# Another order for splits, first step and routing in a decoder-layer kernel, and a scratch of running sums whose half steps are 8 KB pieces

## What is computed

```
proj = x @ W_in.T                      # val, gate, B, C (32 heads x 128), dt (32)
dt = softplus(dt + dt_bias);  ld = dt * -exp(A_log);  cum = cumsum(ld, axis=1)
M = (C @ B.T) * exp(where(mask, cum_l - cum_m, -inf))
Y = M @ val + ... + D * val;  out = (Y * silu(gate)) @ W_out.T
```

```
scores = sigmoid(xt @ gate.T);  _, sel = top_k(scores + expert_bias, 2)
hs = silu(xt @ shared_w1.T) * (xt @ shared_w3.T);  out = hs @ shared_w2.T  (+ routed experts)
```

## Time and profile before

| | |
|---|---|
| median of 3 runs | 790.55 us (790.09 to 791.51) |
| the profiled execution: its own time | 791.8 us |
| the profiled execution: its span | 789.9 us |
| PE busy | 740.9 us (94%) |
| DVE busy | 578.2 us (73%) |
| ACT busy | 455.0 us (58%) |
| POOL busy | 353.6 us (45%) |
| mean granted PE clock | 0.970 |

### The profile page before, as it was taken

One profiled execution on the slowest core, in us unless ns is written; L12 is line 12 of the kernel. 1 busy time (PEld: TensorE's weight loads), 2 busy tenths in 40 slices (PEclk: granted clock), 3 DMA queues, 4 the chain that ended last, 5 costly groups with the idle time before them and its releaser, 6 DMA issues. The chain is left out here.

```text
span 789.9 us, 17296 instructions
## 1 busy us (share of the span) xinstructions
PE 740.9 (94%) x5910; PEld 409.1 (52%) x5918; DVE 578.2 (73%) x1127; ACT 455.0 (58%) x890; POOL 353.6 (45%) x412
## 2 busy tenths in 40 slices
PE   8799599999999999999999999999589999888996
PEld 3455265555655556555565555656324444344554
DVE  5586376686776867868668688796688899847776
ACT  7554155754454664444475554555347788647775
POOL 3864435493342745434358675454213311230343
PEclk9999799999999999999999999999879999889999
DMA  6755114113632232621313334330040000000001
GB/s 208 268 114 178 26 47 90 54 53 78 172 82 53 53 86 51 155 94 53 92 49 99 56 68 104 63 74 2 14 190 15 23 22 23 14 2 1 28 28 54
DMA packets 34282, 57.91 MB, mean 73 GB/s; under 512 B 7040, under 2 KB 11904, under 8 KB 33664
## 3 DMA queue, kind: packets, MB, share of 16 engines
q1 hardware_dynamic: 33664, 57.08, 27.3%
q10 hardware_dynamic: 576, 0.31, 0.1%
HBM read 54.10 MB, written 2.36 MB: 71 GB/s over the span
## 5 line engine op out<-in xcount | busy, mean ns | idle before, releaser
L287 POOL TENSOR_TENSOR cum_rows<-cum_rows,cum_t 128x512 f32<-128x512 f32 x128 | 136.3, 1075 | 205.9 <-DMA cum_rows<-cum_scratch 205.9
L786 PE MATMUL pring<-xt_hi,w_hi 128*128 (+1 forms) x576 | 173.2, 383 | 10.1 <-POOL xt_lo L279 9.0
L786 PE MATMUL pring<-xt_lo,w_hi 128*128 (+1 forms) x576 | 172.5, 381 | 0.0
L786 PE MATMUL pring<-xt_hi,w_lo 128*128 (+1 forms) x576 | 172.2, 381 | 0.0
L647 DVE TENSOR_TENSOR bt<-pring,bt 128x512 f16<-128x512 f32 x128 | 88.1, 689 | 73.9 <-ACT bt L444 73.6
L444 ACT CAST bt<-pring 128x512 f16<-128x512 f32 x128 | 74.7, 584 | 112.7 <-PE pring L786 112.7
L651 DVE TENSOR_TENSOR ct<-pring,ct 128x512 f16<-128x512 f32 x128 | 88.3, 690 | 53.6 <-ACT ct L448 53.1
L828 PEld LDWEIGHTS pscore<-ct,bt 128*128 128x128 f16 x1536 | 96.5, 98 | 32.9 <-issue 5.5
L828 PE MATMUL pscore<-ct,bt 128*128 128x128 f16 x1536 | 107.3, 220 | 1.5 <-issue 1.4
L448 ACT CAST ct<-pring 128x512 f16<-128x512 f32 x128 | 74.9, 585 | 53.0 <-PE pring L786 52.9
L1127 DVE TENSOR_REDUCE mx<-bank_at 128x4 f32<-128x512 f32 x128 | 83.6, 689 | 15.8 <-PE bank_at L1203 14.7
(11 more groups left out here) (153 smaller groups left out, 953.9 us busy)
## 6 DMA issues: line engine op xcount, KB each, us to landing
cum_rows<-cum_scratch SPq DMA_DIRECT2D x32, 1024.0 KB, 8.2
w_raw<-in_w_in SPq DMA_DIRECT2D x35, 256.0 KB, 6.6
q_rows<-in_xt SPq DMA_DIRECT2D x4, 512.0 KB, 11.0
acc<-in_x SPq DMA_DIRECT2D x1, 2048.0 KB, 7.3
vals<-in_vals SPq DMA_DIRECT2D x16, 128.0 KB, 2.1
out<-acc SPq DMA_DIRECT2D x8, 256.0 KB, 2.1
w_raw_e<-in_w_up SPq DMA_DIRECT2D x1, 1024.0 KB, 5.0
w_raw_e<-in_w_gate SPq DMA_DIRECT2D x1, 1024.0 KB, 7.0
```

Source lines behind the costliest of these rows:

```text
L287: nc.gpsimd.tensor_tensor(rows[:, par, :, q], rows[:, par, :, q], own, ALU.subtract).then_inc(sem("since"), 1)
L786: mm = nc.tensor.matmul(bank[name][:], w[:, c, k, cols], x[:, k, bass.ds(n % TB, 1), :].rearrange("p o n -> p (o n)"), start=(i == 0), sto ...
```

## The change

On the host nothing changes. In the kernel these things do:

- The scratch has another layout: block, half step, sequence, head, position. A half step's rows are then one contiguous piece of 8 KB, where they were four pieces of 2 KB. It is stored by 4 transfers per block, one for each sequence (16 in all), where it was stored by 2 transfers in all.
- SP issues the stores of blocks 1 to 3 ahead of the load of `acc` (2 MB), no longer waits for `rows1` there, and waits for all stores.
- Weight chunk 1 is split by ACT (high part only) and DVE (`first_low`), as chunk 0 was; ACT does so ahead of the softplus. POOL takes chunk 5 ahead of the first exponents.
- In the first step PE does pair 0 ahead of the turn of the sums, and pair 3 ahead of the widths of blocks 1 and 2; the width of block 3 comes behind `turn_values`. ACT and DVE have another order of the same work.
- POOL's `split_x(3)` stands ahead of `exponents(2, 0)`.
- In the experts, PE turns the logits ahead of `shared_up(0, 1)`, and DVE's `gate_shared(0)` stands in the middle of the routing.

```diff
-        cum_d = nc.dram_tensor("cum_scratch", (TB, NB * H, L), F32, kind="Internal").ap()
+        cum_d = nc.dram_tensor("cum_scratch", (TB, 2 * GROUPS, NB, 4, L), F32, kind="Internal").ap()
...
             def store_sums(t0, t1):
-                sp.dma_start(cum_d[t0:t1].rearrange("t p n -> p t n"),
-                             dz[:, 0, t0 * L:t1 * L].rearrange("p (t n) -> p t n", n=L)).then_inc(sem("cum_out"), 16)
+                for t in range(t0, t1):
+                    for b in range(NB):
+                        sp.dma_start(cum_d[t, :, b].rearrange("g q n -> g (q n)"),
+                                     dz[b * H:b * H + H, 0, t * L:t * L + L]).then_inc(sem("cum_out"), 16)
             def load_rows(tb, quad, par):
-                src = cum_d[bass.ds(tb, 1)].rearrange("t (b h) n -> (t b) h n", h=H)[:, bass.ds(4 * quad, 4), :]
-                sp.dma_start(rows[:, par].rearrange("p b q n -> p b (q n)"),
-                             src.rearrange("b q n -> b (q n)").partition_broadcast(P)).then_inc(sem(f"rows{par}"), 16)
+                src = cum_d[bass.ds(tb, 1), bass.ds(quad, 1)].rearrange("t g b q n -> (t g) (b q n)")
+                sp.dma_start(rows[:, par].rearrange("p b q n -> p (b q n)"),
+                             src.rearrange("o n -> (o n)").partition_broadcast(P)).then_inc(sem(f"rows{par}"), 16)
             sp.wait_ge(sem("dt_cum"), 1)
             store_sums(0, 1)
-            sp.wait_ge(sem("cum_out"), 16)
+            sp.wait_ge(sem("cum_out"), 16 * NB)
...
-            sp.wait_ge(sem("rows1"), 16)
+            sp.wait_ge(sem("dt_cum"), TB)
+            store_sums(1, TB)
             sp.dma_start(acc[:], io["x"]).then_inc(sem("in_x"), 16)
             sp.dma_start(expo[:], io["expo"]).then_inc(sem("in_x"), 16)
-            sp.wait_ge(sem("dt_cum"), TB)
-            store_sums(1, TB)
-            sp.wait_ge(sem("cum_out"), 32)
+            sp.wait_ge(sem("cum_out"), 16 * NB * TB)
...
-            pool.wait_ge(sem("w_ready"), 1)
-            for c in range(1, 5):
+            pool.wait_ge(sem("w_ready"), 2)
+            for c in range(2, 6):
                 lo_part(0, c)
             pool.wait_ge(sem("cum_t"), 1)
-            exponents(0, 0, {1: 5, 3: 6})
+            exponents(0, 0, {3: 6})
...
             split_x(2)
+            split_x(3)
             exponents(2, 0)
-            split_x(3)
...
             split_x(0)
             hi_part(0, 0, True)
+            hi_part(0, 1, True)
...
             softplus(slice(0, L), 0)
-            hi_part(0, 1, True)
             hi_part(0, 2, True)
...
+            def first_low(c):
+                dve.wait_ge(sem("w_hi"), c + 1)
+                nc.vector.scalar_tensor_tensor(out=w_lo[:, c], in0=w_raw[:, c], scalar=W_SCALE, in1=w_hi[:, c], op0=ALU.mult, op1=ALU.subtract).then_inc(sem("w_ready"), 1)
...
                 project(0, "gate", 0, 1, "gate_proj")
+                pair(0, 0)
                 turn_sums(0, 1)
-                pair(0, 0)
                 pair(0, 1)
                 scores(0, 0)
                 pair(0, 2)
                 scores(0, 1)
-                for t in range(1, TB):
-                    step_widths(t)
                 pair(0, 3)
+                step_widths(1)
+                step_widths(2)
                 scores(0, 2)
                 turn_values(0)
+                step_widths(3)
...
                 if r == 0:
+                    gate_shared(0)
                     routed(nc.vector.scalar_tensor_tensor(out=biased[:], in0=chosen[:, 0], scalar=NEVER, in1=biased[:], op0=ALU.mult, op1=ALU.add))
...
-            shared_up(0, 1)
             pe.wait_ge(sem("lg"), 1)
             for b in range(NB):
                 mm = nc.tensor.transpose(px[1][:, b * L:b * L + L], lg[:, b * L:b * L + L], ident[:])
             mm.then_inc(sem("lg_turn"), 1)
+            shared_up(0, 1)
```

More of the change, by code:

```diff
@@ L404, in hi_part @@
                         act.wait_ge(sem("c_proj"), (TB * g - 1) * SLOTS + c)
-                if first and c == 0:
+                if first and c < 2:
                     nc.scalar.mul(w_hi[:, c], w_raw[:, c], W_SCALE).then_inc(sem("w_hi"), 1)
@@ L476, in first_step @@
                 evac_c(0, 2)
-                decays(0, 0)
                 hi_part(0, 6, True)
                 evac_b(0, 3)
-                decays(0, 1)
+                hi_part(0, 7, True)
                 evac_c(0, 3)
-                decays(0, 2)
-                hi_part(0, 7, True)
-                evac_b(0, 4)
-                decays(0, 3)
+                hi_part(0, 8, True)
+                for e in range(3):
+                    decays(0, e)
                 act.wait_ge(sem("dt_mm"), TB)
                 softplus(slice(L, TOK), 3)
+                evac_b(0, 4)
                 evac_c(0, 4)
-                hi_part(0, 8, True)
+                decays(0, 3)
                 evac_b(0, 5)
+                evac_c(0, 5)
                 decays(0, 4)
-                evac_c(0, 5)
-                decays(0, 5)
                 act.wait_ge(sem("in_wo"), 32)
@@ L496, in first_step @@
                 evac_b(0, 6)
+                decays(0, 5)
                 evac_c(0, 6)
@@ L594, in _ @@
             split_x(0)
[L595 to L596 removed]
+            def first_low(c):
+                dve.wait_ge(sem("w_hi"), c + 1)
+                nc.vector.scalar_tensor_tensor(out=w_lo[:, c], in0=w_raw[:, c], scalar=W_SCALE, in1=w_hi[:, c], op0=ALU.mult, op1=ALU.subtract).then_inc(sem("w_ready"), 1)
+            first_low(0)
             dve.wait_ge(sem("in_dtb"), 32)
@@ L691, in first_step @@
                     convolve(0, k)
-                sums_turned(0, 1)
                 gate_silu(0)
                 low_b(0, 0)
+                low_c(0, 0)
+                sums_turned(0, 1)
                 val_silu(0)
-                low_c(0, 0)
-                for s in (1, 2):
+                for s in (1, 2, 3):
                     low_b(0, s)
@@ L700, in first_step @@
                 weigh(0, 0)
-                low_b(0, 3)
                 weigh(0, 1)
-                low_c(0, 3)
+                pad_values(0)
                 weigh(0, 2)
-                pad_values(0)
-                low_b(0, 4)
-                weigh(0, 3)
                 step_sizes(slice(L, TOK), 3)
                 rates(slice(L, TOK), 3)
+                sums(1)
+                low_b(0, 4)
+                sums(2)
                 low_c(0, 4)
-                for t in range(1, TB):
-                    sums(t)
+                sums(3)
+                weigh(0, 3)
                 low_b(0, 5)
@@ L1477, in _, with gate_shared @@
             nc.vector.tensor_tensor(s_down_parts[:, 1], s_down[:], s_down_parts[:, 0], ALU.subtract).then_inc(sem("s_down_lo"), 1)
+            def gate_shared(t):
+                j, par = turn(f"S{t}"), turn(f"S{t}") % 2
+                dve.wait_ge(sem("gate_mm"), j + 1)
+                dve.wait_ge(sem("act"), silus_before(f"S{t}") + 1)
+                if t >= 2:
+                    dve.wait_ge(sem("hid_lo"), t - 1)
+                nc.vector.tensor_tensor(hid_s[:, t % 2], act_s[:, par], pb[par][:], ALU.mult).then_inc(sem("shared_hid"), 1)
             dve.wait_ge(sem("score"), 1)
@@ L1500, in _ @@
             nc.vector.tensor_tensor(weight[:], chosen[:, 0], score[:], ALU.mult).then_inc(sem("weight"), 1)
-            def gate_shared(t):
-                j, par = turn(f"S{t}"), turn(f"S{t}") % 2
-                dve.wait_ge(sem("gate_mm"), j + 1)
-                dve.wait_ge(sem("act"), silus_before(f"S{t}") + 1)
-                if t >= 2:
-                    dve.wait_ge(sem("hid_lo"), t - 1)
-                nc.vector.tensor_tensor(hid_s[:, t % 2], act_s[:, par], pb[par][:], ALU.mult).then_inc(sem("shared_hid"), 1)
             def low_hidden(t):
@@ L1546, in final_rows @@
                     nc.vector.tensor_scalar(acc[:, b], acc[:, b], mean_var3[:, b, 0:1], rstd3[:, b:b + 1], ALU.subtract, ALU.mult).then_inc(sem("final"), 1)
-            gate_shared(0)
             gate_shared(1)
```

5 lines of the change are left out of this document (2 added, 3 removed).

## The result

Four executions of the changed kernel had a median of 786.08 us (784.80 to 788.35), four of the kernel before 790.89 (790.09 to 791.51): ratio 0.9943, 95% interval 0.9918 to 0.9968. It is faster by 4.8 us where 15.35 were forecast; the range of 771.5 to 779.5 does not hold it. The profiled execution is the slowest of the four, with a time of its own of 788.35 and a span of 786.5.

A forecast was written before the change was run, and what follows sets the result against it. PE was taken as the bound, through its waits and slow-clock spells. Terms 9.0 + 2.35 + 3.0 + 1.0 = 15.35 us off the 790.55 median gave 775.2 us, range 771.5 to 779.5.

The forecast's parts named there:

- Step 2's start: PE's start of step 2: earlier `split_x(3)` removes its 9.0 us wait, and the slow clock behind it, 2.35 us.
- No other engine took PE's place: At step 2's start, a rival: another engine close behind PE becomes the limit, 789 to 791 us, chance 0.03.
- First step: PE's losses in the first step fall from 7.3 us to 3.3 to 4.1; -3.0 taken, bounds -0.5 and -4.0.
- The list of losses before: PE in the first step: 1.13 low part, 3.5 x, 1.7 slow clock, 1.0 ahead of `scores`; sum 7.3 us.
- The rows: Step 1's row load behind stores and `acc`: lands at 52 to 55, wanted at 54.4; cost 0, bound +2 us.
- Rival (2) (*Less*): Late `rows(1,0)` make `weigh(1, 0)` wait 3 us, or first step gains only 0.5: 777.5 to 781 us, chance 0.20.
- the prediction's own signs of being wrong: New profile: step 1 waits for rows, landings over 10 us, stores over 0.5 us apart, or new slow-clock spells.
- The Trainium skill's rule cited in the prediction: On the sixteen stores: merge small transfers; about 2.0 us each in turn would give some 800 us.
- transfers served in turn: A rival on the sixteen stores: each takes its 1.5 us landing one after another, 792.5 us, chance 0.03.
- "It hardly matters": Row-load landing time in later steps: POOL's long waits for rows lie under PE's work, with some 19 us allowed.
- The landing time taken (7.5): A row load in one 8 KB piece: bounded by 5.0 and 8.2 us, 7.5 taken because the shared address stays.
- Routing, -1.0: In the experts, lg's transposes start at about 709.9 instead of 710.89, moving DVE's chain: -1.0 us, bounds 0 and -2.0.

The follow-up runs named there:

- split_only: The kernel before with only `split_x(3)` moved ahead of `exponents(2, 0)`: 781.05 us, ratio 0.9870.
- late_all: The changed kernel with acc and expo loaded right behind wo, each block stored once scanned, and every row load of `next_rows` one slot (4.1 us) later: 781.67 us.
- routing_only: The kernel before with the edits of the experts' routing alone: 789.68 us, ratio 0.9975.
- old_routing: The changed kernel with the experts' routing of before: 790.53 us, ratio 0.9975.
- old_scratch: The changed kernel with the scratch, two stores and row load of before, all orders kept as changed: 777.38 us, ratio 0.9831.
- old_scratch_old_routing: The old_scratch kernel with the experts' routing of before as well: 776.92 us.
- after_again: The changed kernel run once more, unchanged, as a control: 785.75 us.

## Why the prediction was wrong, step by step

**Step 2's start, -9.0 and -2.35: right.** `split_only` shows both in place (11.56 us in the trace, 10.2 in the median). No other engine took PE's place.

**First step, -3.0: right in kind, 0.7 too much.** In after step 1 starts at 45.23 instead of 47.49, -2.26. The pair's wait and those for x went, and `scores(0,2)` waits 2.33 us, as worked out. The slow clock came back behind it (0.54 from 28 to 31). The list of losses before also counted some idle time twice: of the 6 us put down to the slow clock PE was busy 4.76, and the rest is waits for x, which stand in the list by themselves.

**The rows, 0 with bound +2: this step failed.** It reads: "`weigh(1, 0)`, moved up by three us, wants them at 54.4. So it is covered, or short by less than a microsecond". Three things were wrong in it. The largest is the waiter: ACT comes to the rows before DVE does, because `decays(1,0)` stand ahead of `evac_b(1,1)` and `evac_c(1,1)`, which PE needs for its next scores, so they were due between 51 and 52 and not at 54.4. Already in before they were just in time: ACT came from `decays(1,0)` to `evac_b(1,1)` 0.16 us before PE had filled the bank. Second, a store issue was priced by six weight loads and one store at 0.40; these took 0.72, twelve of them 3.8 us more than the 4.8 put down. Third, the landing: 52 to 55 was forecast, 56.8 measured, 46.84 plus the 4.7 of a load plus what was left of `acc` (5.2 us more than that load alone). Together 5.1 us of idle time and 2.5 of slow clock: 7.6. Rival (2) (*Less*) had the late rows at 58 and 3 us of wait; it was the right mechanism with the wrong waiter and half the price. Two of the prediction's own signs of being wrong came: the wait in step 1, and stores spread at more than 0.5 us each. The Trainium skill's rule cited in the prediction (page "DMA: Bandwidth & Descriptors", section "Rules for kernel authors": transfers under 64 KB mostly pay overhead) pointed the right way: the layout with its sixteen stores costs 8.7 us. But it does so not as transfers served in turn (twelve issues took 8.6 us, not 18): the stores cost by their place in SP's queue, and some of the 8.7 is the drift told next. The fixed part of about 2.0 us stands on that page of the Trainium skill for transfers issued from GpSimd; here SP issues, and the 64 KB store of before lands in 1.5.

**"It hardly matters" that rows land sooner: wrong as well.** The slack of POOL was read as room without a price. The rows that landed 3.5 us early moved POOL's exponents onto DVE's work on y, 1.5 us from step 2 to 15 in after, none in `late_all`. In step 0 PE stood 7.5 and 7.7 us in two profiled executions, behind an operation of DVE that lasted until POOL paused. The landing time taken (7.5) was too long as well, 4.7 measured: the four pieces, or the distance between them, were the reason (no run tells the two apart), while the prediction had ruled out the number of pieces by the weight loads' pieces of 2 KB and had kept the shared address as the reason.

**Routing, -1.0: the order works as told, its price is open.** The transposes of lg start at 708.32, 0.64 behind the start of its copy (1.66 in the earlier trace rows). The medians of the three pairs give 2.4 (`routing_only`), 4.5 (`old_routing`, which its trace does not put on the routing) and -0.5 us for it (`old_scratch` and `old_scratch_old_routing`, run on two chips). The tail, from step 15's transpose to the end of the span, varies from 250 to 256 us between profiles, with slow-clock spells in attention and experts, and a value of 1 can't be told in it.

**The sum.** Forecast 15.35; the profiled executions differ by 3.45. The missing 11.9 are 7.6 (step 1) and 0.7 (first step), less 0.3 that step 2's start gained beyond its term, 1.5 of drift, and 2.4 behind step 15, where no cause was traced: the tail of `after_again`, the same kernel, is 3.3 us shorter (251.26 against 254.53), so most of this term may belong to that one execution and not to the kernel. The medians differ by 4.8. With the old scratch the same orders give 13.9.

## What to carry to other kernels

Where a load comes later, look for its first waiter in every queue, and count what stands behind that waiter on its engine: here ACT's in-order queue made rows due some 3 us before the time worked out from the instruction that multiplies by them. Many small transfers on one queue cost first the issues ahead of the next urgent one. A wait of an engine that is off the critical path may be what keeps it clear of another engine; shortening it should be priced like any added work.

## What was not expected of the hardware

- A broadcast read of one 8 KB piece by 128 partitions lands in 4.7 us (223 GB/s), of four pieces of 2 KB, 16 KB apart, in 8.2.
- A store from 32 partitions with 512 B each took SP 0.72 to 0.77 us to issue, one from all 128 partitions 0.35 to 0.40.
- DVE's operation from SBUF to SBUF took 5.81 and 5.87 us instead of 0.4 to 1.4 in two profiled executions, ending in both some 0.2 us behind the beginning of POOL's first gap. In `after` it took 1.40 us with POOL's instructions just as close; in the profiles with pauses given, 0.69 and 0.42. In `after` DVE's operation on y was held up by one instruction of POOL at most (1.53 us instead of 0.68). The page "SBUF — State Buffer" of the Trainium skill, section "SBUF: two separate sides", says that the two engines share a pair of ports, which one holds for a whole instruction while the other is blocked. The traces agree on the blocking (1.53 us on y, through to the end of POOL's instruction and 0.55 more); they show more than it, a hold-up across seven of POOL's instructions. What decides whether DVE gets in between two of them stays open.
